# Two graph layers on one core: the heads' denominators folded to 64 partitions, high and low part in one product

## The chip, the cores and the metric

One NeuronCore of a Trainium2 chip. The metric is the device time of one execution in microseconds, the median over runs.

## The reference, cut to what matters

The kernel computes a graph attention network of two layers, a normalisation, a graph convolution of two layers and a second normalisation, for 1024 nodes with 768 features. The change lies in the first attention layer, which has 8 heads:

```python
h = (x @ W).reshape(n, H, C)                              # 8 heads of 768
e = leaky_relu(alpha_s[src] + alpha_d[dst], NEG_SLOPE)
e = exp(e - segment_max(e, dst)[dst])
denom = segment_sum(e, dst)
alpha = e / (denom[dst] + EPS)
out = segment_sum(h[src] * alpha[:, :, None], dst)
...
h = elu(h)                                                # then the second layer's x @ W2
```

In the kernel the weights `e` of one head are a dense matrix, source node by destination node, with the number of edges as a factor. A denominator is the sum of such a matrix over the source nodes.

## The kernel before, in words

An fp32 value is split into a high part rounded to `float32r` and a low part, the rest. A product of two such values is three TensorE matmuls, high x high, high x low and low x high (`split_products`, lines 38 to 43; in the profile L41, L42 and L43).

After the first stage (x times the first weights, until 484 us) come 16 **units** u = 0 to 15 (`U = 2 * H`): head u mod 8 for the first 512 destination nodes in units 0 to 7, for the other 512 in units 8 to 15. A unit is, on TensorE, six **gathers** (`gather(u, k)`, k = 0 to 5: 128 of the head's 768 features times the weights, 8 source blocks x 3 matmuls of 128x512 into bank 6 or 7) and six **projections** (`project(u, k)`: the result of a gather, now in `hh` and `hl`, times a slice of the second layer's weights in `w2h` and `w2l`, 18 matmuls of 128x512). The order on each engine is written out by hand in one loop over u per engine. For TensorE (lines 1622 to 1664) it is gathers 0, 1, 2, projection 0, gather 3, projection 1, gather 4, projection 2, gather 5, projection 3, **the denominator's product**, projections 4 and 5. Where `u % H == 0` (units 0 and 8) all of gathers 0 to 4 come before projection 0, since the banks of the projections are taken.

While unit u runs, VectorE and ScalarE make the weights of the next one, v = u + 1, in 8 blocks i of 128 source nodes: ScalarE's `exponentials` (L625, L626), VectorE's `weights` (L1013, L1019, into `pf`), ScalarE's `weight_high` (L634, into `ph`), VectorE's `weight_low` (L1024, into `pl`) and `sum_rows` (L1032, L1037), which adds the blocks into `psum_rows` [128, 512]; for v = 0 GpSimd does most of these sums (L568). Between them stands the treatment of the current unit's gathers, tile g = 6u + k: VectorE's `average` (L1106: bank times `rden`, into `mean`), ScalarE's `bend` (L684, L685, into `he` and `hr`), VectorE's `head_sum` (L1110), ScalarE's `head_high` (L691, into `hh`), VectorE's `head_low` (L1115, into `hl`). The slices of the second weights are split by ScalarE's `second_high` (L676, into `w2h`) and VectorE's `second_low` (L1045, into `w2l`).

The denominator needs the sum of `psum_rows` over the partitions, on every partition, which is a product with a 128x128 block of ones. The last steps for v are:

- ScalarE `sum_high(v)` (lines 708 to 714): after the seventh sum of rows, cast `psum_rows` into `psum_h`.
- VectorE `sum_low(v)` (lines 1039 to 1041): `psum_l = psum_rows - psum_h`.
- TensorE `sum_weights(v, bank)` (lines 1617 to 1620): two matmuls, ones with `psum_h` and ones with `psum_l`.
- VectorE `inverse(v, bank)` (L1052): the reciprocal into `rden`; gather 0 of unit v waits for it.

For v = 0 the product stands right behind gather 0 of unit 0, in bank 0; for each other v behind projection 3 of unit u = v - 1, in bank 6. In units 0 to 14 the order near the end of a unit is:

```python
# ScalarE, lines 789 to 794           # VectorE, lines 1310 to 1323
head_high(g + 4)                      head_low(g + 4)
sum_high(v)                           sum_rows(v, 7)
second_high(g + 5)                    sum_low(v)
bend(g + 5)                           second_low(g + 5)
head_high(g + 5)                      average(g + 5)
                                      head_sum(g + 5)
                                      head_low(g + 5)
                                      second_low(g + 6)
                                      inverse(v, banks[6])
```

Engines wait on counting semaphores; an instruction that waits holds up all behind it on its engine. SyncE issues the DMAs; of them only that of `mask2`, in the last unit, waits for a semaphore that the change renames.

Of the kernel before, what the change touches and what calls it, by code (L numbers as in the profile page):

```python
# [120 lines left out]
def graph_and_layers(nc, sem, put, psum, banks, t):  # L121
# [77 lines left out]
    mean = put("mean", 45056, [P, 2, HALF], F32)  # L199
    w2h = put("w2h", 102400, [P, 3, D], F32R)  # L200
    w2l = put("w2l", 111616, [P, 3, D], F32R)
    psum_h = put("psum_h", 120832, [P, HALF], F32R)
    psum_l = put("psum_l", 122880, [P, HALF], F32R)
    e1 = put("e1", 126976, [P, 2, HALF], F32)
    e2 = put("e2", 131072, [P, 2, HALF], F32)
    psum_rows = put("psum_rows", 135168, [P, HALF], F32)
# [60 lines left out]

    row_in, mask_in, top_sum, expo_step, expo_saved, expo_in = (sem(n) for n in ("row_in", "mask_in", "top_sum", "expo_step", "expo_saved", "expo_in"))
    e_done, e_max, p_full, p_hi, p_lo, p_sum = (sem(n) for n in ("e_done", "e_max", "p_full", "p_hi", "p_lo", "p_sum"))
    sum_hi, sum_lo, den_full, rden_done = sem("sum_hi"), sem("sum_lo"), sem("den_full"), sem("rden_done")  # L270
    hc_in = [sem(f"hc_in{i}") for i in range(3)]
    w2_in = [sem(f"w2_in{i}") for i in range(3)]
    w2_hi, w2_lo = sem("w2_hi"), sem("w2_lo")
# [83 lines left out]
    with nc.Block() as block:  # L357
        @block.sync
        def _(sp):
# [109 lines left out]
            for u in range(U):  # L469
# [11 lines left out]
                for k in range(FB):  # L481
# [16 lines left out]
                    if u == U - 1 and k == 1:  # L498

                        sp.wait_ge(den_full, U)  # L500
                        sp.wait_ge(e_max, U * NB)
                        sp.wait_ge(sum_lo, U)
                        sp.dma_start(mask2[:, :, :].rearrange("p b n -> p (b n)"), mask_d).then_inc(mask2_in, 16)
                    if u == U - 1 and k == 3:
                        sp.wait_ge(logit2_sum, logits2_by(HNB - 1, 0))
# [71 lines left out]
        def _(act):  # L577
# [92 lines left out]
            def second_high(g):  # L670
                act.wait_ge(w2_in[g % 3], 16 * (g // 3 + 1))
                if g == 0:
                    act.wait_ge(main_full, STEPS)
                elif g >= 3:
                    act.wait_ge(c_used, g - 2)
                nc.scalar.copy(w2h[:, g % 3, :], w2r[:, g % 3, :]).then_inc(w2_hi, 1)  # L676
# [28 lines left out]
                act.wait_ge(rows_turned, 1)  # L705
                nc.scalar.copy(rows[i][:, :, CW:D], banks[1 + 3 * i][:, :].rearrange("p (c f) -> p c f", c=2)).then_inc(rows_out, 1)

            def sum_high(v):
                act.wait_ge(p_sum, v * 7 + 7)
                if v == 0:  # L710
                    act.wait_ge(main_full, STEPS)
                if v == H + 1:
                    act.wait_ge(rows_saved[1], 16)
                nc.scalar.copy(psum_h[:, :], psum_rows[:, :]).then_inc(sum_hi, 1)

            def early_high(b):
                act.wait_ge(h2_in[b // 2], 16)
                nc.scalar.copy(gh[0][:, b, 0:D], h2r[:, b, :]).then_inc(g_hi, 1)

            sum_high(0)  # L720
            for u in range(U):
                v, g = u + 1, u * FB
# [65 lines left out]
                    weight_high(v, 7)  # L788
                head_high(g + 4)
                if more:  # L790
                    sum_high(v)
                second_high(g + 5)
                bend(g + 5)
                head_high(g + 5)
                if more:
# [68 lines left out]
        def _(dve):  # L864
# [103 lines left out]
            def logits_of(m):  # L968

                dve.wait_ge(part_sum, parts_before[3 * (m + 1) * NB])  # L970
                hs = slice(2 * m, 2 * m + 2)
                both = [[logit_parts[:, :, hs, k, part].rearrange("p b h -> p h b") for part in range(2)] for k in range(2)]
                nc.vector.tensor_tensor(src_logit[:, hs, :], both[0][0], both[0][1], ALU.add).then_inc(logit_sum, 1)
                nc.vector.tensor_tensor(dst_logit[:, hs, :], both[1][0], both[1][1], ALU.add).then_inc(logit_sum, 1)
                dve.wait_ge(logit_sum, 3 * m + 1)
                nc.vector.tensor_scalar(src_logit02[:, hs, :], src_logit[:, hs, :], SLOPE, None, ALU.mult).then_inc(logit_sum, 1)
# [49 lines left out]
            def sum_rows(v, i):  # L1026

                if i == 1:
                    dve.wait_ge(p_full, v * NB + 2)
                    if v >= 1:  # L1030
                        dve.wait_ge(sum_lo, v)
                    nc.vector.scalar_tensor_tensor(out=psum_rows[:, :], in0=pf[:, 0, :], scalar=DEN_EPS / P, in1=pf[:, 1, :],  # L1032
                                                   op0=ALU.add, op1=ALU.add).then_inc(p_sum, 1)
                else:
                    dve.wait_ge(p_full, v * NB + i + 1)
                    dve.wait_ge(p_sum, v * 7 + i - 1)
                    nc.vector.tensor_tensor(psum_rows[:, :], psum_rows[:, :], pf[:, i % 2, :], ALU.add).then_inc(p_sum, 1)  # L1037

            def sum_low(v):
                dve.wait_ge(sum_hi, v + 1)  # L1040
                nc.vector.tensor_tensor(psum_l[:, :], psum_rows[:, :], psum_h[:, :].bitcast(F32), ALU.subtract).then_inc(sum_lo, 1)

            def second_low(g):
                dve.wait_ge(w2_hi, g + 1)
# [47 lines left out]
                            weight_low(0, b - 1)  # L1092
            weight_low(0, NB - 1)
            logits_of(3)
            sum_low(0)
            inverse(0, banks[0])
            logits_turned(3, banks[1])
# [115 lines left out]
            for u in range(U):  # L1213
# [96 lines left out]
                head_low(g + 4)  # L1310
                if more:
                    sum_rows(v, 7)
                    sum_low(v)
                second_low(g + 5)
                if not more:
                    row_low(2)
                    row_low(3)
                average(g + 5)
                head_sum(g + 5)
                head_low(g + 5)  # L1320
                if more:
# [116 lines left out]
        def _(pe):  # L1438
# [176 lines left out]
                return last  # L1615

            def sum_weights(v, bank):
                pe.wait_ge(sum_lo, v + 1)
                nc.tensor.matmul(bank[:, :], ones_r[:, :], psum_h[:, :], start=True, stop=False)
                nc.tensor.matmul(bank[:, :], ones_r[:, :], psum_l[:, :], start=False, stop=True).then_inc(den_full, 1)  # L1620

            for u in range(U):
                v = u + 1
# [545 lines left out]
```

## Time and profile before

| | |
|---|---|
| Median of 3 runs | 1687.92 us (1686.45 to 1688.25) |
| The profiled execution's own time | 1686.97 us |
| Its span, first to last instruction | 1685.2 us |
| TensorE matmuls | 7549 |
| VectorE busy | 1207.2 us, 72% |
| ScalarE busy | 788.7 us, 47% |
| GpSimd busy | 154.7 us, 9% |
| Mean granted TensorE clock | 0.998 |

Read it from the engine with the largest share downwards, and then stage by stage: a share over the whole span says nothing about one unit. The mean duration of a matmul is from its start to the arrival of its last result, and the next one starts long before that, so that the distance between starts is the measure of what one takes. PE is TensorE, PEld its weight loads, DVE VectorE, ACT ScalarE, POOL GpSimd, SP SyncE.

### The profile page before, as it was taken

What the parts mean: (1) busy time and instruction counts of PE and PEld (TensorE: products, weight loads), DVE (VectorE), ACT (ScalarE), POOL (GpSimd) and SP (SyncE); (2) the same over time, 40 slices, a digit from 0 to 9 for tenths busy, and PEclk for the clock granted to TensorE, in tenths of its full rate; (3) what the DMA queues carried; (4) which work ended last, traced back from release to release, by engine and by line L of the source; (5) the groups of instructions that cost most, each with busy time, mean ns of one, the idle gap of its engine ahead of it and who ended that gap; (6) DMA issues with size and microseconds to landing.
All of it is one profiled execution on the core that took longest, in us unless ns stands there. A gap on an engine that the chain in (4) does not pass through costs nothing. (4 is left out here: it accounts for less than half of the span.)

```text
span 1685.2 us, 21615 instructions
## 1 busy us (share of the span) xinstructions
PE 1655.7 (98%) x7549; PEld 1388.8 (82%) x7549; DVE 1207.2 (72%) x2347; ACT 788.7 (47%) x1258; POOL 154.7 (9%) x126
## 2 busy tenths in 40 slices
PE   7899999999999999999999999999999999999998
PEld 6688888888877888888888888888888887988898
DVE  8844456654698887887788688878886858786447
ACT  5233332222455654665556556545655535554340
POOL 0022222221210000000000000000000001032003
PEclk9999999999999999999999999999999999999999
DMA  4156557865563764576566557645753546123122
GB/s 168 49 179 197 189 182 176 228 229 183 190 219 138 206 172 132 185 197 155 180 188 166 200 134 216 165 131 182 197 148 144 216 167 169 29 98 103 57 91 98
DMA packets 135327, 271.83 MB, mean 161 GB/s; under 512 B 24234, under 2 KB 83508, under 8 KB 122676
## 3 DMA queue, kind: packets, MB, share of 16 engines
q1 hardware_dynamic: 134068, 267.29, 51.7%
q0 software_dynamic: 1152, 3.15, 1.0%
q8 instruction: 63, 1.03, 0.3%
q14 instruction: 44, 0.36, 0.1%
HBM read 210.01 MB, written 60.40 MB: 160 GB/s over the span
## 5 line engine op out<-in xcount | busy, mean ns | idle before, releaser
L41 PE MATMUL psum<-ph,hc 128*128 128x512 f32 x768 | 299.5, 390 | 2.2 <-DVE pl L1024 1.2
L42 PE MATMUL psum<-pl,hc 128*128 128x512 f32 x768 | 298.8, 389 | 0.0
L43 PE MATMUL psum<-ph,hc 128*128 128x512 f32 x768 | 298.8, 389 | 0.0
L963 DVE CUSTOM_DVE_ANT_0 junk<-psum,a_bc 128x512 bf16<-128x512 f32 (+1 forms) x256 | 130.0, 555 | 183.1 <-ACT st L616 167.5
L41 PE MATMUL psum<-wh,xTh 128*128 128x512 f32 x570 | 222.8, 391 | 0.0
L43 PE MATMUL psum<-wh,xTl 128*128 128x512 f32 x570 | 221.9, 389 | 0.0
L42 PE MATMUL psum<-wl,xTh 128*128 128x512 f32 x570 | 221.9, 389 | 0.0
L616 ACT CAST st<-psum 128x512 fp32r<-128x512 f32 x96 | 56.6, 589 | 275.4 <-PE psum L43 256.1
L41 PEld LDWEIGHTS psum<-ph,hc 128*128 128x128 f32 x768 | 144.2, 188 | 34.3 <-issue 2.3
L43 PEld LDWEIGHTS psum<-ph,hc 128*128 128x128 f32 x768 | 144.2, 188 | 29.9
L42 PEld LDWEIGHTS psum<-pl,hc 128*128 128x128 f32 x768 | 144.2, 188 | 29.6
L684 ACT ACTIVATE he<-mean,bias 128x512 f32<-128x512 f32 x96 | 69.7, 726 | 210.7 <-DVE mean L1106 210.7
L43 PE MATMUL psum<-w2h,hl 128*128 128x512 f32 x384 | 149.5, 389 | 0.0
L41 PE MATMUL psum<-w2h,hh 128*128 128x512 f32 x384 | 149.5, 389 | 0.0
L42 PE MATMUL psum<-w2l,hh 128*128 128x512 f32 x384 | 149.4, 389 | 0.0
L43 PEld LDWEIGHTS psum<-wh,xTl 128*128 128x128 f32 x570 | 107.0, 188 | 22.3
L41 PEld LDWEIGHTS psum<-wh,xTh 128*128 128x128 f32 x570 | 107.0, 188 | 22.2
L42 PEld LDWEIGHTS psum<-wl,xTh 128*128 128x128 f32 x570 | 107.0, 188 | 22.0
L1106 DVE TENSOR_TENSOR mean<-psum,rden 128x512 f32<-128x512 f32 x96 | 65.9, 686 | 69.2 <-PE psum L43 69.2
L634 ACT CAST ph<-pf 128x512 fp32r<-128x512 f32 x128 | 79.7, 623 | 75.9 <-DVE pf L1019 75.9
L676 ACT CAST w2h<-w2r 128x768 fp32r<-128x768 f32 x96 | 79.5, 830 | 70.7 <-PE psum L43 70.7
L563 POOL TENSOR_TENSOR wl<-wr,wh 128x512 fp32r<-128x512 f32 x66 | 87.0, 1318 | 268.6 <-ACT wh L580 268.6
(288 smaller groups left out, 3144.6 us busy)
## 6 DMA issues: line engine op xcount, KB each, us to landing
hc<-h_scratch SPq DMA_DIRECT2D x96, 1024.0 KB, 5.8
h_scratch<-st SPq DMA_DIRECT2D x96, 512.0 KB, 3.1
w2r<-in_L_gnn_W SPq DMA_DIRECT2D x96, 384.0 KB, 6.7
wr<-in_L_gnn_W SPq DMA_DIRECT2D x12, 1536.0 KB, 8.4
gwr<-in_L_gnn_W SPq DMA_DIRECT2D x24, 384.0 KB, 3.3
row_bc<-logits_scratch SPq DMA_DIRECT2D x16, 512.0 KB, 12.5
expo_bc<-expo_scratch SPq DMA_DIRECT2D x16, 512.0 KB, 6.3
xr<-in_x SPq DMA_DIRECT2D x2, 1536.0 KB, 8.3
```

Of the source, the lines that this page charges most:

```text
L41: nc.tensor.matmul(out, sh, mh, start=first, stop=False, skip_group_check=not grouped)
L42: nc.tensor.matmul(out, sh, ml, start=False, stop=False, skip_group_check=not grouped)
L43: return nc.tensor.matmul(out, sl, mh, start=False, stop=last, skip_group_check=not grouped)
L563: nc.gpsimd.tensor_tensor(wl[i][:, f, :], wr[i][:, f, :], wh[i][:, f, :].bitcast(F32), ALU.subtract).then_inc(w_lo, 1)
L616: nc.scalar.copy(st[n % 4][:, :, 0, :], banks[n % 6][:, :].rearrange("p (g c) -> p g c", g=4)).then_inc(main_hi, 1)
L634: nc.scalar.copy(ph[v % 2][:, i, :], pf[:, i % 2, :]).then_inc(p_hi, 1)
L676: nc.scalar.copy(w2h[:, g % 3, :], w2r[:, g % 3, :]).then_inc(w2_hi, 1)
L684: nc.scalar.activation(he[:, g % 2, :], mean[:, g % 2, :], ACT.Exp, bias=b)
L963: nc.vector.tensor_tensor_reduce(out=junk[:, s % 2, 0:hi - lo], in0=banks[n % 6][:, lo:hi], in1=a_bc[q % 2][:, k, lo:hi], scale=1.0, scala ...
L1106: nc.vector.tensor_tensor(mean[:, g % 2, :], banks[6 + g % 2][:, :], rden[:, :], ALU.mult).then_inc(a_out, 1)
```

## The change

`psum_h` and `psum_l` are replaced by one tile `psum_hl` [128, 512] and a tile `fold` [64, 512]. ScalarE copies partitions 64 to 127 of `psum_rows` into `fold` (`fold_rows`), VectorE adds them to partitions 0 to 63 (`fold_sums`), ScalarE casts the 64 sums into the upper half of `psum_hl` (`sum_high`), VectorE writes the rest into its lower half (`sum_low`), and one matmul with ones takes both. On ScalarE `fold_rows` has the place that `sum_high` had, and `sum_high` stands behind `second_high(g + 5)`. On VectorE `fold_sums` stands behind `second_low(g + 5)`, and `sum_low` behind `average(g + 5)`. For v = 0 the four steps follow one another. Every other line is as it was.

```diff
-    psum_h = put("psum_h", 120832, [P, HALF], F32R)
-    psum_l = put("psum_l", 122880, [P, HALF], F32R)
+    psum_hl = put("psum_hl", 120832, [P, HALF], F32R)
+    fold = put("fold", 122880, [P // 2, HALF], F32)
...
-                        sp.wait_ge(sum_lo, U)
+                        sp.wait_ge(sum_step, 2 * U)
...
-            def sum_high(v):
+            def fold_rows(v):
                 act.wait_ge(p_sum, v * 7 + 7)
                 if v == 0:
                     act.wait_ge(main_full, STEPS)
                 if v == H + 1:
                     act.wait_ge(rows_saved[1], 16)
-                nc.scalar.copy(psum_h[:, :], psum_rows[:, :]).then_inc(sum_hi, 1)
+                nc.scalar.copy(fold[:, :], psum_rows[P // 2:P, :]).then_inc(sum_copied, 1)
+
+            def sum_high(v):
+                act.wait_ge(sum_step, 2 * v + 1)
+                if v >= 1:
+                    act.wait_ge(den_full, v)
+                nc.scalar.copy(psum_hl[0:P // 2, :], psum_rows[0:P // 2, :]).then_inc(sum_copied, 1)
...
+            fold_rows(0)
             sum_high(0)
...
                 head_high(g + 4)
                 if more:
+                    fold_rows(v)
+                second_high(g + 5)
+                if more:
                     sum_high(v)
-                second_high(g + 5)
                 bend(g + 5)
...
-                        dve.wait_ge(sum_lo, v)
+                        dve.wait_ge(sum_step, 2 * v)
...
+            def fold_sums(v):
+                dve.wait_ge(sum_copied, 2 * v + 1)
+                nc.vector.tensor_tensor(psum_rows[0:P // 2, :], psum_rows[0:P // 2, :], fold[:, :], ALU.add).then_inc(sum_step, 1)
+
             def sum_low(v):
-                dve.wait_ge(sum_hi, v + 1)
-                nc.vector.tensor_tensor(psum_l[:, :], psum_rows[:, :], psum_h[:, :].bitcast(F32), ALU.subtract).then_inc(sum_lo, 1)
+                dve.wait_ge(sum_copied, 2 * v + 2)
+                nc.vector.tensor_tensor(psum_hl[P // 2:P, :], psum_rows[0:P // 2, :], psum_hl[0:P // 2, :].bitcast(F32), ALU.subtract).then_inc(sum_step, 1)
...
             logits_of(3)
+            fold_sums(0)
             sum_low(0)
...
                     sum_rows(v, 7)
-                    sum_low(v)
                 second_low(g + 5)
+                if more:
+                    fold_sums(v)
                 if not more:
                     row_low(2)
                     row_low(3)
                 average(g + 5)
+                if more:
+                    sum_low(v)
                 head_sum(g + 5)
...
             def sum_weights(v, bank):
-                pe.wait_ge(sum_lo, v + 1)
-                nc.tensor.matmul(bank[:, :], ones_r[:, :], psum_h[:, :], start=True, stop=False)
-                nc.tensor.matmul(bank[:, :], ones_r[:, :], psum_l[:, :], start=False, stop=True).then_inc(den_full, 1)
+                pe.wait_ge(sum_step, 2 * v + 2)
+                nc.tensor.matmul(bank[:, :], ones_r[:, :], psum_hl[:, :], start=True, stop=True).then_inc(den_full, 1)
```

## Rows read from the trace of the kernel before

**Rows 1.** The page's first part: busy time, share of the span, instructions.

```profile
PE 1655.7 (98%) x7549; PEld 1388.8 (82%) x7549; DVE 1207.2 (72%) x2347; ACT 788.7 (47%) x1258; POOL 154.7 (9%) x126
```

**Rows 2.** TensorE's waits, 500 to 1400 us: total, times, longest.

```profile
PE psum L41 <- DVE mean L1106: 0.8, 1, 0.8
PE psum L41 <- DVE hl L1115: 0.7, 2, 0.4
```

**Rows 3.** Busy time by stretch: length, busy us of each engine, PEclk, DMA share, GB/s.

```profile
485.00:532.70 47.70, 44.37 (x194) 35.82 (x193) 43.81 (x67) 28.56 (x44) 0.00 (x0) 1.00 0.48 173
532.70:540.00 7.30, 6.92 (x29) 5.47 (x30) 5.07 (x6) 5.03 (x8) 0.00 (x0) 1.00 0.81 328
540.00:943.00 403.00, 403.00 (x1777) 333.37 (x1776) 328.01 (x485) 225.94 (x341) 0.00 (x0) 1.00 0.60 172
...
1003.00:1400.00 397.00, 397.00 (x1751) 328.36 (x1750) 304.78 (x457) 211.36 (x317) 0.00 (x0) 1.00 0.55 168
```

**Rows 4.** TensorE's timeline, unit 8: start, duration, instruction, idle before.

```profile
995.39 0.40 PE L1619 MATMUL psum<-psum_h,ones_r 128*128 128x512 f32 x1
995.62 0.40 PE L1620 MATMUL psum<-psum_l,ones_r 128*128 128x512 f32 x1
...
1000.40 0.47 PE L41 MATMUL psum<-hh,w2h 128*128 128x512 f32 x1 [0.29 <-DVE hl L1115]
```

**Rows 5.** Timeline of all engines at denominator 0.

```profile
482.92 0.62 ACT L714 CAST psum_h<-psum_rows 128x512 fp32r<-128x512 f32 x1 [1.13 <-POOL psum_rows L568]
...
483.65 0.68 DVE L1041 TENSOR_TENSOR psum_l<-psum_rows,psum_h 128x512 fp32r<-128x512 f32 x1
...
484.48 0.48 PE L1619 MATMUL psum<-psum_h,ones_r 128*128 128x512 f32 x1
...
484.79 0.40 PE L1620 MATMUL psum<-psum_l,ones_r 128*128 128x512 f32 x1
```

**Rows 6.** Timelines of ScalarE, VectorE and TensorE in unit 0.

```profile
531.76 0.83 ACT L676 CAST w2h<-w2r 128x768 fp32r<-128x768 f32 x1
...
532.62 0.96 DVE L1045 TENSOR_TENSOR w2l<-w2r,w2h 128x768 fp32r<-128x768 f32 x1
533.49 0.68 DVE L1106 TENSOR_TENSOR mean<-psum,rden 128x512 f32<-128x512 f32 x1
...
532.72 0.47 PE L1619 MATMUL psum<-psum_h,ones_r 128*128 128x512 f32 x1 [2.36 <-DVE psum_l L1041]
537.90 0.47 PE L41 MATMUL psum<-hh,w2h 128*128 128x512 f32 x1 [0.36 <-DVE hl L1115]
```

**Rows 7.** VectorE's timeline in unit 8.

```profile
994.38 0.69 DVE L1041 TENSOR_TENSOR psum_l<-psum_rows,psum_h 128x512 fp32r<-128x512 f32 x1 [0.69 <-ACT psum_h L714]
```

**Rows 8.** Timelines of VectorE and TensorE in a common unit, unit 5.

```profile
815.08 0.96 DVE L1045 TENSOR_TENSOR w2l<-w2r,w2h 128x768 fp32r<-128x768 f32 x1
817.74 0.69 DVE L1106 TENSOR_TENSOR mean<-psum,rden 128x512 f32<-128x512 f32 x1 [1.70 <-PE psum L43]
...
821.63 0.39 PE L1619 MATMUL psum<-psum_h,ones_r 128*128 128x512 f32 x1
```

**Rows 9.** Groups by shape: partitions x elements, count, busy us, mean ns.

```profile
L591 ACT CAST key<-psum 128x128 int16<-128x128 f32 x1 | 0.3, 267 | 3.8 <-PE psum L1442 3.8
L667 ACT COPY dinvT<-psum 8x128 f32<-8x128 f32 x1 | 0.3, 251 | 0.0
...
L982 DVE COPY logitT<-psum 16x128 f32<-16x128 f32 x4 | 1.0, 256 | 0.0
```

**Rows 10.** TensorE's wait at 1410 us, and stretches of 2 us (columns as rows 3).

```profile
1410.42 0.32 PE L1668 MATMUL psum<-ident,logit 128*128 128x128 f32 x1 [1.62 <-DVE logit L1136]
...
1412.00:1414.00 2.00, 1.75 (x6) 1.12 (x5) 2.00 (x7) 2.00 (x6) 2.00 (x3) 0.71 1.08 207
1414.00:1416.00 2.00, 1.85 (x8) 1.13 (x7) 1.86 (x10) 0.86 (x3) 0.46 (x1) 0.50 1.09 210
1416.00:1418.00 2.00, 2.00 (x12) 1.75 (x11) 1.38 (x3) 1.75 (x4) 0.00 (x0) 0.94 1.08 207
```

More of the change, by code:

```diff
@@ L269, in graph_and_layers @@
     e_done, e_max, p_full, p_hi, p_lo, p_sum = (sem(n) for n in ("e_done", "e_max", "p_full", "p_hi", "p_lo", "p_sum"))
-    sum_hi, sum_lo, den_full, rden_done = sem("sum_hi"), sem("sum_lo"), sem("den_full"), sem("rden_done")
+    sum_copied, sum_step, den_full, rden_done = sem("sum_copied"), sem("sum_step"), sem("den_full"), sem("rden_done")
     hc_in = [sem(f"hc_in{i}") for i in range(3)]
```

## The prediction

> **What bounds the kernel now.** I read the page first: TensorE is busy for 98% of the span [rows 1]. That could still hide gaps, so next came its waits. Over the whole middle of the kernel it hardly waits at all; what there is, is for VectorE's `mean` and `hl` [rows 2]. Busy times by stretch say the same: from 540 to 943 us and from 1003 to 1400 us TensorE never stops, while VectorE has about a fifth to a quarter of the time free [rows 3]. Only the first unit, 485 to 532.7 us, looks different: VectorE is busy for 43.8 of 47.7 us, and TensorE is not full. So units 1 to 7 and 9 to 14 are worth what TensorE is given to do, and unit 0 is worth what VectorE's order of work is. The third look is at the timeline around each denominator product, since the change rewrites what stands ahead of it. The `mean ns` of a matmul, 390, is not its price: two products of one kind start 0.23 us apart [rows 4], and that is what a removed one gives back.
>
> There are 16 denominators, v = 0 to 15. The first is summed at the very start of unit 0, each other one (v = u + 1) inside unit u. Unit 15 has none.
>
> **Term 1: the product that goes.** One 128x512 product less per denominator: 0.23 us [rows 4] where TensorE is never kept waiting around it. I count 13 such denominators: those of units 1 to 7 and 9 to 14. 13 x 0.23 = **3.0 us gained**. The three others are costed whole below.
>
> **Term 2: the chain that gets longer.** Before, ScalarE copies (0.62 us), VectorE subtracts (0.69 us), TensorE starts 0.15 us after that. After, it is copy, add, copy, subtract, with a hand-over at each step. What do instructions on 64 partitions cost? The trace has none of 64x512. ScalarE's copy of 8x128 took 251 ns and of 128x128 267 ns, VectorE's of 16x128 256 ns [rows 9]: the partitions hardly count, the 512 elements do. So I take the full 0.62 and 0.69 us [rows 5]; the low end, if 64 partitions took half, is 0.31 and 0.35 us, and it goes into the range.
>
> *In a common unit* it is covered. In the unit around 815 us VectorE starts `w2l` at 815.08 and then idles for 1.70 us until the `mean` of the last tile, at 817.74 us. The fold runs in that gap, 816.0 to 816.7, and ScalarE's second copy ends at 817.3. The subtraction comes behind `mean`, where VectorE has nothing to do until ScalarE's exponentials are through. The stack would be ready at about 819.1 us, and TensorE asks for it at 821.63 us [rows 8]: 2.4 us to spare. Cost nothing; if that cover were gone it would be 2.9 us a unit, as in unit 8 below. VectorE and ScalarE get some 10 us more work each over the 16, all in their idle time.
>
> *Denominator 0* has no cover. POOL's last sum ends, ScalarE copies at 482.92, VectorE subtracts at 483.65, TensorE starts at 484.48 us [rows 5]. Now: copy to 483.54; add 483.65 to 484.34; copy 484.37 to 484.99; subtract 485.02 to 485.71; TensorE at 485.86. That is 1.38 us later, and the step from the start of one product to the next just after a wait, 0.31 us (484.48 to 484.79), is saved: **1.1 us lost**. The reciprocal moves with it, and so does all of VectorE's work in unit 0, which runs almost without a pause and on which TensorE waits for `mean` (0.8 us [rows 2]).
>
> *Unit 0.* Here TensorE already stands still: its product at 532.72 us has an idle time of 2.36 us before it, spent on `psum_l` [rows 6]. The change moves this subtraction to behind two things that used to follow it. ScalarE's `w2h` cast ends at 532.59, so VectorE's `w2l` starts at about 532.69 (before: 532.62). It takes 0.87 us until the next can start; the fold starts at 533.56, `mean` at 534.16 (before: 533.49). ScalarE's second copy can start when the fold is through, 534.29, and ends at 534.91; the subtraction runs from 534.97 to 535.66, and TensorE starts at 535.78 in place of 532.72: 3.1 us more. Queued behind the subtraction on VectorE are `head_sum` and `head_low`, which come 0.7 us later because `mean` and ScalarE's exponential do. Before, TensorE lost time for exactly that `hl`, 0.36 us as the row has it, ahead of its product at 537.90 [rows 6]. Now it arrives there at 535.78 + 0.31 + 18 x 0.228 = 540.2, well after `hl` (about 538.5). So at this point the loss is 540.2 - 537.9, less 0.07 for the slower restart that falls away: **2.2 us lost**. The reciprocal ends near 542.8 and TensorE asks for it at 544.3: covered.
>
> *Unit 8* repeats the order of unit 0 (five gathers before the first projection). VectorE's subtraction at 994.38 ends 0.3 us before TensorE wants it at 995.39 [rows 4, 7], and there is the same 0.29 us wait for `hl` at 1000.40. The same chain puts the subtraction's end at 998.15 and TensorE's start at 998.27, 2.9 us later; at 1002.7 it is where it used to be at 1000.40: **2.2 us lost**.
>
> Sum of what can be read: 1.1 + 2.2 + 2.2 - 3.0 = **+2.6 us**.
>
> **Term 3: the clock.** TensorE's stop in unit 0 grows from 2.4 us to 5.4 us of nothing at all, and unit 8 gets one of 2.7 us (998.27 less the end of the product before, 995.55). The trace shows one fall of the granted clock: around 1409 to 1411 us TensorE did almost nothing (one short product between waits, 1.62 us for `logit`), and from 1412 on the clock stood at 0.71, 0.50 and 0.94 in stretches of 2 us, that is at the lower level (1.2 GHz) for 1.16 + 2.0 + 0.24 = 3.4 us [rows 10]. Work under it goes at half speed, so a fall costs at most 1.7 us. After the 2.4 us stop ahead of 532.72 the clock stayed at 1.00 [rows 3]. Bounds for a fall: 0 and 1.7 us each. A stop of 5.4 us is far beyond either case, so I count one fall there; part of the slow stretch may lie within the stop, and I take 1.5 us. The 2.7 us stop lies close to both rows, and I leave it out of the likeliest sum. Behind this stands a row of the Trainium skill ("TensorE: Matmul & The Clock Gate", section "Why this matters for your kernels"), which tells one to leave TensorE no long idle gap between bursts of matmuls, as the clock then drops to its half level; the rows at 1410 us agree. By that rule the sum is +4.1 us, without it +2.6.
>
> On the 64 partitions the Trainium skill ("VectorE: DVE Perf Modes", section on the fixed extra latency of SBUF-source instructions) gives the add a time that depends on elements per partition alone, an estimate of 0.69 us for 512. No row here shows it for 64 partitions; the 128x512 rows agree, and it speaks against the low end above.
>
> **Forecast.** 2.6 + 1.5 = +4.1 us. The profiled execution took 1686.97 us (span 1685.2), 0.95 us under the median of 1687.92; I put the sum on the median: **1692.0 us**, 0.24% slower. A difference of 0.2% (3.4 us) is about what a measurement of this kernel can tell from none.
>
> **Rivals.**
> A. *The clock falls in unit 8 as well*: another 1.6 us, +5.7, 1693.6 us. For it: 2.7 us is longer than the stop which kept the clock. Against: that one was only 0.3 us shorter. Chance 0.30.
> B. *No fall at all*: +2.6 us, 1690.5 us, not to be told from no change. For it: the 2.4 us stop cost nothing. Chance 0.15.
> C. *Not slower: instructions on 64 partitions are cheaper.* Place: the four-step chains of denominator 0 and units 0 and 8. If they take half, denominator 0 costs -0.3 us (same chain, one product less), and in units 0 and 8 the stack is ready 1.2 us sooner: 1.0 us each instead of 2.2. Sum -0.3 + 2.1 - 3.0 = -1.2 us, 1686.7 us. Between full and half length the sum crosses zero at about two thirds of the full length; there the stops also grow too short to touch the clock. Against it: [rows 9]. Chance 0.05.
> D. *The waits are covered everywhere*, for instance because the moved subtraction still comes early in units 0 and 8: 16 x 0.23 = 3.7 us gained, 1684.2 us. Against it: in unit 0 TensorE waits already. Chance 0.04.
> E. *The cover in the common units is thinner than read*, so that some of the 13 wait too: from 2.9 us each. Against it: 2.4 us to spare. Chance 0.03, above 1695 us.
> The forecast itself: 0.43.
>
> **Range and chances.** 1688.9 to 1694.6 us: from below B (its terms may each be off by half a microsecond) to above A (two falls at the full 1.7 us are +6.0). C, D and E are left out. Slower by over 0.2%: A, E and three quarters of the forecast, 0.65. Within 0.2%: B, C and the rest, 0.30. Faster: 0.05.
>
> **What would show it.** In the profile after: one `psum_hl` product for each denominator, 16 products fewer in all; between 540 and 943 us and 1003 and 1400 us still a full TensorE, with units 0.23 us shorter. The waits of TensorE for the subtraction into `psum_hl`: some 1.4 us at denominator 0, 5.4 us in unit 0 and 2.7 us in unit 8, and the waits for `hl` gone. Below-full granted clock within some microseconds after unit 0's stop and perhaps after unit 8's. The 64-partition adds and copies at 0.69 and 0.62 us. Wrong it would be if those are much shorter, if no longer wait stands in units 0 and 8, or if a wait shows in the others.

## The result, and the profile after

The changed kernel takes **1693.08 us** (median of 10 runs, 1692.13 to 1695.29) against 1687.91 (1686.45 to 1689.5) on the same chip: a ratio of 1.0033, 95% interval 1.0025 to 1.0040. It is slower by a third of a per cent, 5.2 us. The forecast was 1692.0; rival A, with a second fall of the clock, was 1693.6 and lies nearer.

First the page of the changed kernel (its first part) and TensorE's waits from 500 to 1400 us, which answer to [rows 1] and [rows 2]:

```profile
PE 1654.4 (98%) x7528; PEld 1388.0 (82%) x7533; DVE 1217.5 (72%) x2363; ACT 799.9 (47%) x1274; POOL 153.9 (9%) x126
```

```profile
PE psum L1638 <- DVE psum_hl L1056: 8.2, 2, 5.5
PE psum L41 <- DVE mean L1122: 0.8, 1, 0.8
```

The busy share says nothing: 98% before and after, and 1.3 us less busy time in a run that is 8 us longer. (The weight loads, PEld, are the 16 fewer that they should be; of the matmuls five more records are missing.) The waits say more. A new one, for the stack's low half, stands there twice with 8.2 us. Before, the denominator's own wait was 2.36 us, in unit 0 alone [rows 6]; the two for `hl` [rows 2] are gone. Nothing else is new in these 900 us, so units 1 to 7 and 9 to 14 pay nothing.

The second reading is TensorE's timeline at the three exposed products (denominator 0, units 0 and 8) and behind them; the bracket is the idle time ahead of the instruction:

```profile
486.59 0.47 PE L1638 MATMUL psum<-psum_hl,ones_r 128*128 128x512 f32 x1 [1.38 <-DVE psum_hl L1056]
...
537.67 0.77 PE L1638 MATMUL psum<-psum_hl,ones_r 128*128 128x512 f32 x1 [5.45 <-DVE psum_hl L1056]
538.23 0.63 PE L41 MATMUL psum<-hh,w2h 128*128 128x512 f32 x1
538.65 0.63 PE L42 MATMUL psum<-hl,w2h 128*128 128x512 f32 x1
...
543.32 0.40 PE L41 MATMUL psum<-w2h,hh 128*128 128x512 f32 x1
543.56 0.40 PE L42 MATMUL psum<-w2l,hh 128*128 128x512 f32 x1
...
544.71 0.39 PE L41 MATMUL psum<-hh,w2h 128*128 128x512 f32 x1
...
1003.14 0.47 PE L1638 MATMUL psum<-psum_hl,ones_r 128*128 128x512 f32 x1 [2.73 <-DVE psum_hl L1056]
1009.18 0.40 PE L41 MATMUL psum<-hh,w2h 128*128 128x512 f32 x1
```

Behind the stop of 5.45 us the products start 0.43 us apart, and from 543.3 us on 0.23 to 0.24 us apart. That is the granted clock, seen in stretches of 2 us (length, busy us of PE, PEld, DVE, ACT and POOL with counts, PEclk, DMA share, GB/s):

```profile
536.00:538.00 2.00, 0.33 (x1) 0.36 (x2) 1.44 (x3) 1.82 (x3) 0.00 (x0) 0.61 1.05 432
538.00:540.00 2.00, 2.00 (x6) 1.54 (x6) 1.06 (x2) 1.24 (x3) 0.00 (x0) 0.50 0.98 403
540.00:542.00 2.00, 2.00 (x6) 1.61 (x5) 1.96 (x3) 0.33 (x1) 0.00 (x0) 0.50 0.35 132
542.00:544.00 2.00, 2.00 (x7) 1.57 (x6) 2.00 (x1) 0.00 (x0) 0.00 (x0) 0.68 0.00 0
...
1004.00:1006.00 2.00, 2.00 (x7) 1.52 (x6) 1.18 (x3) 1.44 (x2) 0.00 (x0) 0.52 0.02 9
1006.00:1008.00 2.00, 2.00 (x7) 1.60 (x6) 2.00 (x2) 0.00 (x0) 0.00 (x0) 0.63 0.00 0
```

A stretch at PEclk 0.61 has spent 0.39 x 2 x 2 = 1.56 us at the lower level (1.2 GHz). Unit 0: 1.56 + 2.0 + 2.0 + 1.28 = 6.8 us, of which 5.6 under work. Unit 8: 1.92 + 1.48 = 3.4 us. In the profiled execution of before, neither place had a fall.

Third, the shapes that the trace of before did not have (groups by shape: partitions x elements, count, busy us, mean ns, idle before), and VectorE's and TensorE's timeline in a common unit, unit 5, which answers to [rows 8]:

```profile
L722 ACT CAST psum_hl<-psum_rows 64x512 fp32r<-64x512 f32 x16 | 9.9, 620 | 25.1 <-DVE psum_rows L1052 25.1
L716 ACT COPY fold<-psum_rows 64x512 f32<-64x512 f32 x16 | 9.9, 619 | 21.5 <-DVE psum_rows L1048 20.4 <-POOL psum_rows L570 1.1
```

```profile
821.68 0.68 DVE L1052 TENSOR_TENSOR psum_rows<-psum_rows,fold 64x512 f32<-64x512 f32 x1
823.33 0.69 DVE L1122 TENSOR_TENSOR mean<-psum,rden 128x512 f32<-128x512 f32 x1 [0.98 <-PE psum L43]
824.06 0.69 DVE L1056 TENSOR_TENSOR psum_hl<-psum_rows,psum_hl 64x512 fp32r<-64x512 f32 x1
...
827.22 0.40 PE L1638 MATMUL psum<-psum_hl,ones_r 128*128 128x512 f32 x1
```

Half the partitions save nothing: 619 and 620 ns for the copies, 677 and 686 ns for VectorE's two. In the common unit the low half is ready at 824.75 us, and TensorE asks for it at 827.2: 2.5 us to spare.

**Where the 8.3 us of the two profiled executions lie** (1695.29 against 1686.97). I cut each trace at two marks on TensorE: the last product that waits for `pl` before denominator 0, and the first transpose of `logit` in unit 15. Before, that stretch is 483.49 to 1410.42 us, 926.9 us long. After, it begins 0.75 us later (the first stage, which the change does not touch) and is 6.56 us longer; the tail behind it adds 0.8 (8.1 us in all by the spans, 1693.3 against 1685.2). Inside it, after taking off the 0.75: at 544.71 the kernel is 6.1 us late against 537.90 before, of which denominator 0 is 1.1; at 1009.18 it is 8.0 us late against 1000.40; and from the product of unit 1 to that of unit 7 it takes (941.96 - 597.76) / 6 = 57.37 us a unit in place of (936.86 - 591.18) / 6 = 57.61, so that a removed product gives back **0.25 us**. These are the four products, two before and two after:

```profile
591.18 0.39 PE L1619 MATMUL psum<-psum_h,ones_r 128*128 128x512 f32 x1
936.86 0.39 PE L1619 MATMUL psum<-psum_h,ones_r 128*128 128x512 f32 x1
...
597.76 0.40 PE L1638 MATMUL psum<-psum_hl,ones_r 128*128 128x512 f32 x1
941.96 0.40 PE L1638 MATMUL psum<-psum_hl,ones_r 128*128 128x512 f32 x1
```

| part, in us | predicted | in this trace |
|---|---|---|
| 13 covered products | -3.0 | -3.25 |
| denominator 0 | +1.1 | +1.1 |
| unit 0, waits | +2.2 | +2.3 |
| unit 0, clock | +1.5 | +2.6 |
| unit 8, waits | +2.2 | +2.1 |
| unit 8, clock | 0 (rival A: 1.6) | +1.6 |
| sum | +4.1 (A: +5.7) | +6.5 |

(The predicted parts as printed add up to +4.0; the recorded sums, +2.6 and +4.1, are 0.1 us too high.) The clock's rows are taken from the time between the exposed product and the first product of projection 5 behind it: 4.44 us at full clock (537.19 to 541.63 in the kernel kept busy, below), 7.04 us in unit 0, 6.04 in unit 8. The profiled run is the slowest of the ten; the medians are 5.2 us apart.

### The profile page after: what moved, and what is told of

It reads as the page before. It is cut to its first block and busy times, and to the rows that moved or that the text cites. A ratio compares the mean times of both kernels' runs of the same rounds, so it can differ in the third digit from the quotient of the medians.

```text
span 1693.3 us, 21625 instructions
## 1 busy us (share of the span) xinstructions
PE 1654.4 (98%) x7528; PEld 1388.0 (82%) x7533; DVE 1217.5 (72%) x2363; ACT 799.9 (47%) x1274; POOL 153.9 (9%) x126
## 5 line engine op out<-in xcount | busy, mean ns | idle before, releaser
L1060 DVE TENSOR_TENSOR w2l<-w2r,w2h 128x768 fp32r<-128x768 f32 x96 | 91.6, 955 | 36.3 <-ACT w2h L678 35.8
```

Of the source, the lines that this page charges most:

```text
L1060: nc.vector.tensor_tensor(w2l[:, g % 3, :], w2r[:, g % 3, :], w2h[:, g % 3, :].bitcast(F32), ALU.subtract).then_inc(w2_lo, 1)
```

## The experiments

The questions: is it the exposed chains and the clock behind them, and in which shares? The rivals: the fold's work slows something else; or the stack itself costs more than a product with two operands. Every run was timed beside the kernel before on its own chip. In the table "stretch" is the difference of the stretch defined above, which leaves out the first stage and the tail; these two vary among the thirteen profiles by up to 2.5 and 3.1 us, whatever the kernel. The tail has a fall of the clock of its own near 1410 us, in ten of the thirteen, of 3.4 us at the lower level in six and of 6.8 us in four; in the first execution of the changed kernel it has none. A profile is one execution and the ratio is over all of them, so the two need not agree to the microsecond.

| kernel | median us | ratio to before, 95% | stretch |
|---|---|---|---|
| after, second time | 1694.48 | 1.0036 (1.0024 to 1.0048) | +5.4 |
| one product alone | 1684.86 | 0.9980 (0.9971 to 0.9989) | -3.4 |
| after, TensorE kept busy | 1689.75 | 1.0011 (1.0002 to 1.0020) | +1.9 |
| fold for 13 | 1685.71 | 0.9983 (0.9974 to 0.9992) | -2.4 |
| after, steps adjacent | 1688.54 | 1.0004 (0.9995 to 1.0013) | +1.3 |
| after, product later | 1691.80 | 1.0011 (1.0000 to 1.0022) | -0.3 |
| fold for 13, `mean` first | 1686.49 | 0.9982 (0.9974 to 0.9991) | -4.2 |
| after, denominator 0 whole | 1696.05 | 1.0034 (1.0021 to 1.0048) | +7.2 |
| fold for 13, both moves | 1687.70 | 0.9988 (0.9977 to 0.9998) | -3.3 |
| before, kept busy | 1688.17 | 0.9998 (0.9989 to 1.0007) | +0.7 |
| fold for 13, `mean` first, kept busy | 1683.23 | 0.9968 (0.9956 to 0.9981) | -4.6 |

**What the product alone is worth.** The kernel before, with `sum_weights` reduced to its first product. The denominators then leave out the low part of the sums.

```diff
-nc.tensor.matmul(bank[:, :], ones_r[:, :], psum_h[:, :], start=True, stop=False)
-nc.tensor.matmul(bank[:, :], ones_r[:, :], psum_l[:, :], start=False, stop=True).then_inc(den_full, 1)
+nc.tensor.matmul(bank[:, :], ones_r[:, :], psum_h[:, :], start=True, stop=True).then_inc(den_full, 1)
```

> The kernel before with one product per denominator, ones with psum_h; the low part is left out of the denominators, everything else (its subtraction and the wait for it too) stays. It measures what a removed product is worth. Theory of the prediction: 0.23 us in each of 13 units, 0.3 at denominator 0, nothing in units 0 and 8, where the wait for hl takes it up: -3.3 us against the kernel before, about 1684.6. Rival 1, a product is worth its 0.39 us of busy time: -6.2 us. Rival 2, the common units are not set by TensorE alone, and a product removed there gives nothing: 0.

Measured: 0.9980, stretch -3.4 us. What the change can bring is there, without its price. In units 0 and 8 the product saved is partly taken up by the wait behind it: the wait for `hl` in unit 0 is 0.58 us instead of 0.36, in unit 8 0.53 instead of 0.29.

**The clock.** The changed kernel, with TensorE given idle products (into the same bank, which the real one overwrites) while it would stand still: 21 in unit 0, 10 in unit 8.

```diff
 def sum_weights(v, bank):
+    for i in range({1: 21, H + 1: 10}.get(v, 0)):
+        if i == 0:
+            pe.wait_ge(h_lo, (v - 1) * FB + 5)
+        nc.tensor.matmul(bank[:, :], ones_r[:, :], hh[:, ((v - 1) * FB + 4) % 3, :], start=True, stop=True)
     pe.wait_ge(sum_step, 2 * v + 2)
```

> The changed kernel, with TensorE kept at work in the two pauses: ahead of the wait for psum_hl stand 21 products of ones with hh in unit 0 (4.8 us of a pause of 5.5) and 10 in unit 8 (2.3 of 2.7), into the bank that the denominator's product then starts afresh. It takes the fall of the clock away and leaves the waits. Theory: the granted clock stays at 1.00 at 540 and 1005 us, and against the kernel before the time is only the +2.6 us of the waits, 1690.5; 2.6 us under the changed kernel's 1693.1. Rival 1, the clock has no part in it and the loss is all waiting or all added work on VectorE and ScalarE: 1693.1 as the changed kernel. Rival 2, the clock falls all the same: 1693.

TensorE's timeline and one stretch of it (columns as above), unit 0:

```profile
532.21 5.13 PE L1640 MATMUL psum<-hh,ones_r 128*128 128x512 f32 x21 [0.35 <-DVE hl L1131]
537.19 0.50 PE L1642 MATMUL psum<-psum_hl,ones_r 128*128 128x512 f32 x1
```

```profile
538.00:540.00 2.00, 2.00 (x10) 1.67 (x9) 1.17 (x3) 1.45 (x2) 0.00 (x0) 1.00 0.66 263
```

Ten products lie in the stretch where the changed kernel had six. The denominator's product starts no sooner (537.19 against 537.67, the first stage being 0.4 us earlier here), since VectorE is what it depends on; only the clock is different. The ratio falls from 1.0033 to 1.0011 (the intervals, 1.0025 to 1.0040 and 1.0002 to 1.0020, do not meet): **0.2%, about 3.7 us, is what the clock costs the changed kernel**, and the rest, 1.9 us by the stretch, is the waits less the products. This separates the two, since the chains and the stack are exactly those of the change.

**The exposed chains.** The fold is kept for 13 denominators; v = 0, 1 and 9 take the old copy, subtraction and two products, in their old place.

```diff
+WHOLE = (0, 1, H + 1)
 def fold_rows(v):
-    nc.scalar.copy(fold[:, :], psum_rows[P // 2:P, :]).then_inc(sum_copied, 1)
+    if v in WHOLE:
+        nc.scalar.copy(psum_hl[:, :], psum_rows[:, :]).then_inc(sum_copied, 1)
+    else:
+        nc.scalar.copy(fold[:, :], psum_rows[P // 2:P, :]).then_inc(sum_copied, 1)
...
-nc.tensor.matmul(bank[:, :], ones_r[:, :], psum_hl[:, :], start=True, stop=True).then_inc(den_full, 1)
+last = nc.tensor.matmul(bank[:, :], ones_r[:, :], psum_hl[:, :], start=True, stop=v not in WHOLE)
+if v in WHOLE:
+    last = nc.tensor.matmul(bank[:, :], ones_r[:, :], psum_l[:, :], start=False, stop=True)
+last.then_inc(den_full, 1)
```

> The fold with one product for 13 denominators, the old copy, subtraction and two products in their old places for the three whose chain is exposed (v = 0, 1 and 9). Theory: the 13 give 3.0 us and the three give nothing away: 1684.9 us, the clock as in the kernel before. Rival, added work: the 26 more instructions on VectorE and ScalarE cost in the common units too, so that 13 of 16 parts of the loss remain: 1692. Middle: no difference from before, 1687.9.

Measured: 0.9983, faster than before, so the sign of the change hangs on three denominators of sixteen. Both rivals fall with it: thirteen folds and stacks, with all their added work, leave a gain close to that of the product alone (0.9980). Its profile had one fall of the clock, although the stop was as long as that of before (2.36, [rows 6]). TensorE's timeline and stretches, unit 0:

```profile
533.66 0.52 PE L1656 MATMUL psum<-psum_hl,ones_r 128*128 128x512 f32 x1 [2.34 <-DVE psum_l L1069]
```

```profile
532.00:534.00 2.00, 0.34 (x2) 0.32 (x3) 1.28 (x3) 1.35 (x2) 0.00 (x0) 0.98 1.01 415
534.00:536.00 2.00, 2.00 (x6) 1.61 (x5) 1.11 (x2) 0.85 (x2) 0.00 (x0) 0.50 1.00 405
536.00:538.00 2.00, 2.00 (x7) 1.52 (x7) 0.69 (x2) 1.24 (x3) 0.00 (x0) 0.66 1.08 449
```

A stop of the same 2.34 us stands in the kernel with one product, and there the clock held:

```profile
532.76 0.47 PE L1619 MATMUL psum<-psum_h,ones_r 128*128 128x512 f32 x1 [2.34 <-DVE psum_l L1041]
...
534.00:536.00 2.00, 2.00 (x10) 1.67 (x9) 0.59 (x2) 1.34 (x2) 0.00 (x0) 1.00 1.08 435
```

So a stop of that length stands at an edge: the clock may hold or fall behind it.

**The order.** The changed kernel with the four steps next to each other, so that the fold and the subtraction go ahead of `w2l` on VectorE and the second copy ahead of `w2h` on ScalarE.

```diff
     fold_rows(v)
+    sum_high(v)
 second_high(g + 5)
-if more:
-    sum_high(v)
...
     sum_rows(v, 7)
+    fold_sums(v)
+    sum_low(v)
 second_low(g + 5)
-if more:
-    fold_sums(v)
 average(g + 5)
-if more:
-    sum_low(v)
```

> The changed kernel with the four steps directly behind each other (fold_rows and sum_high ahead of second_high on ScalarE, fold_sums and sum_low ahead of second_low on VectorE). It undoes the order alone. Theory: in units 0 and 8 psum_hl comes 1.4 us later than psum_l did, not 3.1; hl comes 1.4 us later, and that is what TensorE then waits for. 1.1 + 1.4 + 1.4 - 3.0 = +0.9 us, 1688.8; with a pause of 3.7 us in unit 0 the clock may fall once there, up to +2.6 us, 1690.5. The waits for psum_hl in the trace: 1.4, 3.7 and about 1 us. Rival, it is the number of instructions and not the order: as the changed kernel, 1693.1.

TensorE's timeline, units 0 and 8:

```profile
536.21 0.47 PE L1635 MATMUL psum<-psum_hl,ones_r 128*128 128x512 f32 x1 [3.72 <-DVE psum_hl L1055]
...
998.96 0.47 PE L1635 MATMUL psum<-psum_hl,ones_r 128*128 128x512 f32 x1 [0.99 <-DVE psum_hl L1055]
1004.15 0.47 PE L41 MATMUL psum<-hh,w2h 128*128 128x512 f32 x1 [0.64 <-DVE hl L1130]
```

Both stops shrink by 1.7 us, the fall of the clock in unit 8 is gone, that of unit 0 stays (3.4 us at the lower level), and in unit 8 a wait for `hl` takes some of the rest. The ratio is 1.0004. In units 0 and 8 the change as made pays twice, for two more steps and for their late place; neither alone explains the whole.

**Other places for the product and for `mean`.** Two moves in units 0 and 8 alone: TensorE's denominator product behind projection 4, in the changed kernel; and VectorE's `mean` ahead of `w2l`, in the kernel with the fold for 13.

```diff
-    sum_weights(v, banks[6])
+    if u % H:
+        sum_weights(v, banks[6])
     project(u, 4)
+    if u % H == 0:
+        sum_weights(v, banks[6])
```

> The changed kernel with one thing moved: in units 0 and 8 the denominator's product stands behind projection 4 in place of ahead of it. Projection 4 then fills the wait for psum_hl, and the pauses before projection 5 are those for hl. Theory: projection 5 starts when hl is there, 0.7 us later than in the kernel before in unit 0 and 0.6 us in unit 8 (the 2.2 us each are gone but for that); with a product's worth corrected to 0.25 us by the distance of the products in the trace after: 1.1 + 0.7 + 0.6 - 13 x 0.25 = -0.85 us, 1687.1 to 1687.6; pauses of about 1 and 2.3 us in unit 0 and 1.2 in unit 8, the clock at most once low. Rival, the loss is not in these two places (added work, or the 64-partition instructions): as the changed kernel, 1693.

```diff
-second_low(g + 5)
+if u % H:
+    second_low(g + 5)
 average(g + 5)
+if u % H == 0:
+    second_low(g + 5)
```

> The fold for 13 denominators as in e3_fold_13, and in units 0 and 8 VectorE's mean of the last tile ahead of the w2l subtraction and not behind it, so that hl comes 0.87 us sooner. Theory: the waits for hl (0.36 and 0.29 us idle, with the restart 0.5 us each) go, and TensorE keeps the 2.3 us wait for psum_l in unit 0: 13 x 0.25 + 2 x 0.5 = -4.2 us, 0.8 us under e3_fold_13, about 1684.5. Rival: w2l of tile 5, now later, or something else holds projection 5 up just as long: as e3_fold_13.

The later product did what it was to do in the trace. TensorE's waits from 500 to 1400 us with it:

```profile
PE psum L41 <- DVE hl L1131: 4.0, 3, 2.4
PE psum L41 <- DVE mean L1122: 0.8, 1, 0.8
PE psum L1638 <- DVE psum_hl L1056: 0.6, 1, 0.6
```

In unit 0 the stop has been cut into one of 0.64 us for the stack and one of 2.39 us for `hl`, in unit 8 one of 1.22 us for `hl` is left, and no fall follows. The ratio, 1.0011, is 0.2% better than the change, as with the busy TensorE, but its interval reaches from 1.0000 to 1.0022. This chip was less quiet (the kernel before ranged from 1686.9 to 1695.0), and what lies between -0.3 in the stretch and +0.1% in the times I cannot assign. (In the profiled execution the difference from before lies outside the stretch, 1.2 us in the first stage and 2.3 us in the tail, which the edit does not touch.) With the swap nothing is left of the 0.7 us of waits for `hl` in units 0 and 8, the clock holds behind a stop of 2.38 us, and the stretch is -4.2. But in the kernel without the swap the fall of the clock had hidden that wait as well, so the two profiles differ mostly by the fall, and the ratios, 0.9982 and 0.9983, are one. The swap's own worth is not shown.

**Denominator 0 alone, and all moves together.** First the changed kernel with `WHOLE = (0,)`; then the swapped kernel with the later product too.

> The changed kernel with the old chain and two products for denominator 0 alone. It undoes the part that I costed at 1.1 us. Theory: the wait of 1.38 us at 486 us goes, VectorE's work in unit 0 comes 1.1 us sooner, and the waits in units 0 and 8 stay at 5.5 and 2.7 us: 1.1 us under the changed kernel, about 1692.2 where that one has 1693.3. Rival, the first chain is hidden by what follows in unit 0, since TensorE waits there for VectorE anyway: no difference.

> e6_fold_13_swap and, in units 0 and 8, the two products behind projection 4. Theory: the 2.3 us pause for psum_l goes; what TensorE then waits for is hl in unit 0, some 1.7 us with nothing to do. Projection 5 starts 0.3 us earlier than in e6 and the pause is too short to touch the clock, where e3_fold_13 showed a fall behind one of 2.34 us that cost about 1.3 us: -4.5 us against the kernel before, and up to 1.5 more where that one's clock falls; 1683 to 1684. Rival: the clock depends on nothing in unit 0, no gain over e6.

The first is a miss: no gain in the times (1.0034), though an interval of 2.3 us to either side could not have shown 1.1 us. In its trace unit 0's product starts at 536.99 with the first stage 1.19 us late, against 537.67 with 0.75, so 1.1 us sooner as priced. But a new wait in unit 15 of 1.55 us outweighs it. TensorE's row there and VectorE's wait behind which it stands:

```profile
1409.03 0.47 PE L41 MATMUL psum<-hh,w2h 128*128 128x512 f32 x1 [1.55 <-DVE hl L1147]
```

```profile
DVE junk L1206 <- DMA logit_row<-logits_scratch: 5.2, 1, 5.2
```

VectorE waits in its order of work for one DMA of the logits, and `hl` is queued behind it. This wait was 3.2 us before, 3.7 after, 5.2 here and 2.6 to 4.9 in the ten other profiles, none of whose edits touches that transfer. TensorE's wait for `hl` in unit 15 follows it: none up to 3.8 us, then 0.25 us at 3.9, 0.40 at 4.1, 1.2 at 4.9 and 1.55 at 5.2. I take it to belong to the execution and not to the edit, since it can hide a microsecond; no two profiles of one kernel show it at both ends (the changed kernel's two have 3.7 and 3.5 us). The 1.1 us of denominator 0 are thus shown by one trace and not by the times. All moves together are a miss as well: 0.9988 and -3.3 us, with 1.2 us of the same wait in unit 15, and no more than the swap alone.

**Is it the clock in the kernel before, too?** Eight idle products in the stop of unit 0, once in the kernel before and once in the swapped one (the wait and the product as above, with `range(8 if v == 1 else 0)`); and the changed kernel a second time beside them.

> The kernel before, with 8 products of ones with hh (1.9 us) in the 2.36 us stop of unit 0, ahead of its wait for psum_l. e2_keep_busy came out 0.7 us under the sum of its waits, and e3_fold_13 showed a fall of the clock behind a stop of 2.34 us that cost the kernel before nothing in its profile. Theory: the stop of the kernel before is at the edge, its clock falls there in some executions and not in others (1.1 us each time), and with the products in it the time is 0.3 to 1.1 us lower and spreads less: 1687.2. Rival: before, the clock never falls in unit 0; no difference, 1687.9.

> e6_fold_13_swap with the same 8 products in the stop of unit 0. Theory: the waits as in e6 (-4.2 us against the kernel before from the first denominator to the end of unit 15) and no fall in unit 0: 0 to 1 us under e6, 1683.5 on a quiet chip, ratio 0.9975. Rival: the added products hold the denominator's back and cost what they save.

> The changed kernel once more, as the anchor beside the two others, on the same chip and against the same runs of the kernel before. Theory: ratio 1.0030, the same waits of 1.4, 5.5 and 2.7 us for psum_hl, and a fall of the clock in unit 0 in the profile again; in unit 8 it may or may not come. Rival, the fall in unit 0 is by chance: a profile without it.

The times of before show no gain from it (0.9998), but their interval leaves room for up to 1.9 us, more than the 0.3 to 1.1 us of the theory. The mean granted clock, which is on record for every run, says more. On this chip it was 0.9975 in the 17 runs of the kernel before and 0.9985 in the 11 with the idle products. A thousandth of 1686 us is 1.7 us of granted clock, and 3.4 us at the lower level take away just that: one fall. So the kernel before probably does lose the clock behind its 2.36 us stop in many executions, although its profile shows none; that this costs it nothing is not shown, and neither is the place of those falls.

The same numbers give the clock's share in the change. The changed kernel's six runs here have a mean of 0.9957, so against the kernel before it loses 0.0018, which is an estimate of 3.0 us at most. It counts clock and not time: among the runs of one kernel a thousandth less went with 0.8 us more on average over all kernels, and not with 1.7. The two kernels kept busy have nearly the same clock (0.9985 both, on two chips) and ratios of 1.0011 and 0.9998, 2.2 us apart, which is waits less products. That leaves 3.0 of the 5.2 us between the medians to the clock, the same size. The 3.7 us above are more, since they count against a kernel without falls in the middle, and the kernel before is probably not quite that.

The swapped kernel with the idle products has **the lowest ratio of all, 1683.23 us, 0.9968 (0.9956 to 0.9981)**, clear of the two beside it. It is not clear of the swapped kernel without them (0.9974 to 0.9991), so that the idle products' worth in it is not shown. Its waits on TensorE from 490 to 1400 us, and its timeline in unit 0:

```profile
PE psum L41 <- DVE mean L1138: 1.0, 2, 0.8
PE psum L1661 <- DVE hl L1147: 0.4, 1, 0.4
```

```profile
531.16 2.10 PE L1661 MATMUL psum<-hh,ones_r 128*128 128x512 f32 x8 [0.38 <-DVE hl L1147]
533.10 0.44 PE L1663 MATMUL psum<-psum_hl,ones_r 128*128 128x512 f32 x1
```

The changed kernel came out as the first time (1.0036), with waits of 1.39, 5.42 and 2.70 us. In this execution the clock fell three times before the tail, the first time behind denominator 0. TensorE's timeline and stretches:

```profile
487.27 0.77 PE L1638 MATMUL psum<-psum_hl,ones_r 128*128 128x512 f32 x1 [1.39 <-DVE psum_hl L1056]
```

```profile
486.00:488.00 2.00, 0.73 (x3) 0.48 (x3) 0.69 (x1) 2.00 (x4) 0.00 (x0) 0.80 0.97 370
488.00:490.00 2.00, 2.00 (x7) 1.61 (x6) 1.92 (x1) 0.87 (x2) 0.00 (x0) 0.50 1.00 372
...
538.00:540.00 2.00, 1.35 (x3) 1.16 (x4) 1.20 (x2) 1.24 (x3) 0.00 (x0) 0.60 1.05 432
540.00:542.00 2.00, 2.00 (x6) 1.52 (x5) 1.35 (x2) 1.31 (x2) 0.00 (x0) 0.55 0.83 335
```

In unit 0 the lower level lasted 1.6 + 1.8 = 3.4 us this time, not 6.8; in the kernel with denominator 0 whole it was 6.8 us again, behind the same stop of 5.45 us. The number and length of the falls differ from one execution to the next. That this is why the profiled run lies 2 us above the median of its kernel is not shown: its mean clock is 0.996, and of the other nine runs the three at 0.997 took 1692.8 us on average, and those at 0.996 and at 0.995 both 1693.6.

## Why the prediction was right

**The mechanism** was right: products gained where the chain is covered, three exposed chains lost, and the clock on top. Undoing a part moves the time: the clock by 0.2%, the three exposed chains from 1.0033 to 0.9983, and the product alone gives 0.9980. Only the 1.1 us of denominator 0 by itself is not shown by the times.

**Term 1** had the right 13 denominators and a product slightly too cheap: 0.25 us each by the distance between units, not the 0.23 us read from two starts in a row. That is 0.25 us in sum.

**Term 2** held to a tenth: stops of 1.38, 5.45 and 2.73 us where 1.4, 5.4 and 2.7 were forecast, the waits for `hl` gone, 2.5 us to spare in a common unit against 2.4, and its sum 5.5 us. Taken together with term 1 that is +2.5 us, not the +2.6 on record, a slip of rounding that changes nothing. The step that carried it was to write the four hand-overs out with times from the rows. The price of 64 partitions was taken from a small copy, and the new rows bear it out (619 to 620 and 677 to 686 ns); rival C falls with it. The Trainium skill ("VectorE: DVE Perf Modes", section on the fixed extra latency of SBUF-source instructions) gave an estimate of 0.69 us for the add, and the trace has 0.68.

**Term 3** is where the forecast was off. First, "I leave it out of the likeliest sum": the 2.7 us stop of unit 8 was followed by a fall in both profiles of the changed kernel and in that with denominator 0 whole, for 1.6 us in the first of them, which is rival A. Second, "a fall costs at most 1.7 us": this bound was the one fall that the trace of before shows, 3.4 us at the lower level, and in unit 0 the level lasted twice as long and cost 2.6 us. The reasoning that "part of the slow stretch may lie within the stop" held (1.2 of 6.8 us), but the size around it did not. Third, it went by a kernel before that keeps its clock in unit 0, as its one profile shows; over all runs it probably does not always (0.9975 against 0.9985 kept busy), and that worked the other way. In the profiled pair the term measured 4.2 us, over all runs it is some 3 us by the estimates above, where 1.5 was forecast. The sum went to +6.5 in the profiled execution, and the medians to +5.2, inside the range, between the forecast and A and nearer to A. That the forecast was only 1.1 us off is in part luck: the 2.7 us that term 3 lacks in the two units are partly made up by 0.25 us of products and, probably, by falls in the kernel before, which the prediction did not count. The Trainium skill's warning against long idle gaps ("TensorE: Matmul & The Clock Gate", section "Why this matters for your kernels") agrees with the trace at 537 us, where 5.45 us of nothing were followed by a stretch at 0.50. That the clock also fell behind 1.39 and 2.34 us is told by the traces alone.

**D and E** fall with the waits: none is covered in units 0 and 8, and none is new anywhere else between 500 and 1400 us. **B** falls as well, but the kernel kept busy shows that it had about the right size: +1.9 us in the stretch and 1.0011 (0.3 to 3.4 us), where +2.6 was the sum without a fall.

Open: what decides whether the clock falls behind a stop of some 2.4 us (in the profiles it did once, behind 2.34 us, and held behind 2.34, 2.36, 2.38 and 2.39 us); how often it falls there in the kernel before; and how the spread among the executions of the changed kernel, 1692.1 to 1695.3 us, splits between the clock, the first stage and the tail.

## What to carry to other kernels

Read the cover of a longer chain in every kind of unit, not in the common one alone: here 13 of 16 places were free, and the other three set the sign; the edit pays if it is made only where the cover is. On an engine that is otherwise full, price a longer stop with the clock behind it as well, and take the fall shown in a trace as one sample, not as a bound. Where a stop can't be removed, idle work in it can be cheaper than the stop, but only where the clock really falls: it gave the changed kernel 0.2%, and the kernel before nothing that its times show. One profile is one execution; the mean granted clock of all runs helps to tell how often the clock falls.

## What was not expected of the hardware

The granted clock fell behind short stops of TensorE, and not every time. It fell behind all seven stops of 2.70 us or more in the profiles of the middle stages (2.70, 2.73, 2.75, 3.72, 5.42 and twice 5.45 us). Behind 2.34 us it fell once and held once, and it held behind 2.36, 2.38 and 2.39 us. Behind the 1.4 us stop at denominator 0 it fell in one profile (1.39 us, with waits of 0.47 and 0.73 us in the four us before it) and held in four with the same waits.

The lower level lasted 3.4 us in unit 8, in unit 0 of the second execution and in the kernels with 2.34 and 3.72 us, and 6.8 us in unit 0 of the first execution of the same kernel and of the kernel with denominator 0 whole.

And the transfer of the logits in unit 15 kept VectorE waiting from 2.6 to 5.2 us in kernels that do not touch it, at its longest enough to turn into 1.2 to 1.6 us of TensorE's time.
